# Unmasked cross attention: scores and maxima as three one-pass products instead of one fp32 product

## The reference, cut to what matters

```
q = x @ Wq.T + bq
k = context @ Wk.T + bk
v = context @ Wv.T + bv
# split in 16 heads
scores = jnp.einsum('bhtd,bhcd->bhtc', q, k) / jnp.sqrt(d)      # d = 16
attn = jax.nn.softmax(scores, axis=-1)
out = jnp.einsum('bhtc,bhcd->bhtd', attn, v) @ Wo.T + bo
```

## Time and profile before

| | |
|---|---|
| median of 3 runs | 5438.19 us (5427.34 to 5443.7) |
| profiled execution, own time | 5452.68 us |
| its span | 5450.7 us |
| PE busy in the span | 4830.3 us (89%) |
| PE weight loads busy | 3801.2 us (70%) |
| DVE busy | 2680.2 us (49%) |
| ACT (ScalarE) busy | 2135.3 us (39%) |
| POOL (GpSimd) busy | 589.6 us (11%) |
| mean granted TensorE clock | 0.929 of 2.4 GHz |

### The profile page before, as it was taken

How to read it: one execution, slowest core, us unless ns; L and a number is a source line. 1 busy time by engine, 2 the same in 40 slices (tenths; PEclk the granted TensorE clock), 3 DMA queues, 4 the chain that set the end, 5 groups by cost and what they waited for, 6 DMA issues and landing times. The chain is left out here.

```text
span 5450.7 us, 148101 instructions
## 1 busy us (share of the span) xinstructions
PE 4830.3 (89%) x66180; PEld 3801.2 (70%) x66180; DVE 2680.2 (49%) x4650; ACT 2135.3 (39%) x4116; POOL 589.6 (11%) x375
## 2 busy tenths in 40 slices
PE   6999989499999699999886799999459969999968
PEld 5877867388888578887455377877348858888844
DVE  4555545466666445554344255555255545555531
ACT  3554532233333344444021144554225534444430
POOL 1111111000000111110310011110110011111000
PEclk9999985699999899999997899999769989999979
DMA  1111100311111111110000111110101111111000
GB/s 62 39 44 39 39 10 6 89 47 50 50 47 47 50 40 40 40 40 16 32 16 16 35 38 39 39 39 26 22 22 53 51 58 40 40 40 40 22 8 26
DMA packets 82376, 203.70 MB, mean 37 GB/s; under 512 B 26864, under 2 KB 42096, under 8 KB 81760
## 3 DMA queue, kind: packets, MB, share of 16 engines
q1 hardware_dynamic: 81792, 194.79, 11.5%
HBM read 188.06 MB, written 6.70 MB: 36 GB/s over the span
## 5 line engine op out<-in xcount | busy, mean ns | idle before, releaser
L678 DVE TENSOR_REDUCE x_pm<-banks 128x4 f32<-128x1536 f32 (+2 forms) x512 | 935.3, 1827 | 691.7 <-PE banks L581 691.7
L775 ACT ACTIVATE x_pl<-banks 128x384 f32<-128x384 f32 x1536 | 628.8, 498 | 710.8 <-PE banks L564 710.8
L505 POOL TENSOR_TENSOR x_cl<-xnT,x_ch 128x1601 fp32r<-128x1601 f32 x120 | 400.6, 3338 | 3744.5 <-ACT x_ch L790 3744.5
L780 ACT ACTIVATE x_kT<-banks,x_bk 128x384 f32<-128x384 f32 (+2 forms) x512 | 305.1, 596 | 557.0 <-PE banks L592 557.0
L592 PE MATMUL banks<-x_ch,x_wh 128*128 128x384 f32 (+2 forms) x1024 | 409.6, 400 | 92.6 <-POOL x_v L512 89.8
L564 PE MATMUL banks<-x_q,x_kT 32*128 32x128 f32 x13312 | 485.2, 277 | 6.0 <-issue 5.9
L602 PE MATMUL banks<-x_wh,x_ch 128*128 128x256 f32 (+1 forms) x1664 | 489.1, 294 | 0.0
L581 PE MATMUL banks<-x_kT,x_q 32*128 32x384 f32 (+2 forms) x4096 | 456.5, 512 | 13.6 <-DVE x_v L710 8.9
L602 PE MATMUL banks<-x_wh,x_cl 128*128 128x256 f32 (+1 forms) x1664 | 467.8, 281 | 0.0
L602 PE MATMUL banks<-x_wl,x_ch 128*128 128x256 f32 (+1 forms) x1664 | 466.6, 280 | 0.0
L564 PEld LDWEIGHTS banks<-x_q,x_kT 32*128 32x128 f32 x13312 | 438.6, 185 | 9.7 <-issue 7.3
(11 more groups left out here) (349 smaller groups left out, 8300.0 us busy)
## 6 DMA issues: line engine op xcount, KB each, us to landing
xnT<-in_ctxT SPq DMA_DIRECT2D x120, 800.5 KB, 4.4
e_w<-in_L_pack SPq DMA_DIRECT2D x91, 384.0 KB, 3.1
e_w<-in_L_pack SPq DMA_DIRECT2D x56, 320.5 KB, 2.9
actT<-in_ctxT SPq DMA_DIRECT2D x8, 800.5 KB, 7.0
routed_rows<-rw SPq DMA_DIRECT2D x8, 512.0 KB
e_rw<-routed_rows SPq DMA_DIRECT2D x8, 512.0 KB, 8.1
x_side<-mask_rows SPq DMA_DIRECT2D x128, 12.5 KB
x_tok<-in_x SPq DMA_DIRECT2D x1, 1024.0 KB, 5.5
```

The source lines that it names most:

```text
L505: nc.gpsimd.tensor_tensor(cl[:, u, k, 0:CTX], staged(b, k), ch[:, u, k, 0:CTX], ALU.subtract).then_inc(low_done, 1)
L678: nc.vector.tensor_reduce(pm[:, c, :, g], src[:, :, 0:hi - lo], AX.X, ALU.max).then_inc(max_done, 1)
L775: nc.scalar.activation(probabilities(c, j, lo, hi).rearrange("p t q -> p (t q)"), mine[j][:, 0:(hi - lo) * P], ACT.Exp).then_inc(exp_done, 1)
L780: nc.scalar.activation(kT[:, c, lo:hi], mine[1 if g == 0 and inside(b if c else b - 1) else 0][:, 0:hi - lo], ACT.Identity, bias=col[:, c: ...
```

## The change

In unmasked calls, `kT` becomes `kh` and `kl`, and `qb` becomes `qh` and `ql`, all F32R. ScalarE writes `kh` where it wrote `kT`. A new DVE step `take_k` writes `kl` = projected keys + bias - `kh`, from the PSUM bank that ScalarE reads too, after it waited for `k_taken`; it comes right after `take_max` in each cycle, before `divide`, `take_output` and `take_v`. TensorE's `wait_free` waits for the new semaphore `k_low` in place of `k_taken`. `take_q` has four instructions where it had two, the last two wait for the first two. Each score product and each maximum product becomes three, with four strips inside and the three products outside.

```diff
-        kT = net.sb(tag + "_kT", [P, KC, CTX], ctx=mem)
+        if masked:
+            kT = net.sb(tag + "_kT", [P, KC, CTX], ctx=mem)
+        else:
+            kh = net.sb(tag + "_kh", [P, KC, EVEN], F32R, ctx=mem)
+            kl = net.sb(tag + "_kl", [P, KC, EVEN], F32R, ctx=mem)
...
-                after(pe, k_taken, *keys_by(k))
+                after(pe, k_taken if masked else k_low, *keys_by(k))
...
-                    for j in range(4):
-                        r = slice(32 * j, 32 * j + 32)
-                        last = nc.tensor.matmul(sets[g % 2][j][0:n, (t - lo) * P:(t - lo + 1) * P], kT[r, c, t * P:t * P + n],
-                                                qb[r, u, c], start=False, stop=True, skip_group_check=True)
+                    for keys, q in ((kT, qb),) if masked else ((kh, qh), (kh, ql), (kl, qh)):
+                        for j in range(4):
+                            r = slice(32 * j, 32 * j + 32)
+                            last = nc.tensor.matmul(sets[g % 2][j][0:n, (t - lo) * P:(t - lo + 1) * P],
+                                                    keys[r, c, t * P:t * P + n], q[r, u, c], start=False, stop=True,
+                                                    skip_group_check=True)
...
+                else:
+                    even = hi + hi % 2
+                    for n, (q, keys) in enumerate(((qh, kh), (ql, kh), (qh, kl))):
+                        for j in range(4):
+                            r = slice(32 * j, 32 * j + 32)
+                            last = nc.tensor.matmul(into[j][:, 0:even - lo], q[r, u, c], keys[r, c, lo:even], start=(n == 0),
+                                                    stop=(n == 2))
...
+            def take_k(unit, c, g, bank):
+                lo, hi = KEYS[g]
+                hi += hi % 2
+                dve.wait_ge(k_taken, unit + 1)
+                nc.vector.scalar_tensor_tensor(kl[:, c, lo:hi], bank[:, 0:hi - lo], col[:, c:c + 1], kh[:, c, lo:hi], ALU.add,
+                                               ALU.subtract).then_inc(k_low, 1)
+
             def take_q(b, u):
+                if not masked:
+                    src = qT[:, :, bass.ds(b * S, S)]
+                    for e in range(2):
+                        nc.vector.tensor_scalar(qh[:, u, :, e * S:(e + 1) * S], src, net.parity[:, 12 + e:13 + e], None,
+                                                ALU.mult).then_inc(q_staged, 1)
+                    for e in range(2):
+                        dve.wait_ge(q_staged, 4 * b + e + 1)
+                        nc.vector.scalar_tensor_tensor(ql[:, u, :, e * S:(e + 1) * S], src, net.parity[:, 12 + e:13 + e],
+                                                       qh[:, u, :, e * S:(e + 1) * S], ALU.mult,
+                                                       ALU.subtract).then_inc(q_staged, 1)
+                    return
...
+                        if not masked and inside(b + 1):
+                            take_k(k + 8, c, g, mine[1 if g == 0 and inside(pb) else 0])
                         if g == 1 and c == 0 and inside(b - 1):
                             divide(b - 1, mine[3])
```

More of the change, by code:

```diff
@@ L383, in cross_attention @@
     names = ("w_in bias_in raw_in0 raw_in1 w_high w_low high_done low_done pad_set mask_in0 mask_in1 side_set shift_set "
-             "sums_set q_staged m_full max_done z_step z_ready z_turned nm_ready s_full exp_done k_full k_taken v_full "
+             "sums_set q_staged m_full max_done z_step z_ready z_turned nm_ready s_full exp_done k_full k_taken k_low v_full "
              "v_taken pv_full o_taken den_full inverted out_ready")
@@ L388, in cross_attention @@
             side_set, shift_set, sums_set, q_staged, m_full, max_done, z_step, z_ready, z_turned, nm_ready, s_full,
-            exp_done, k_full, k_taken, v_full, v_taken, pv_full, o_taken, den_full, inverted, out_ready):
+            exp_done, k_full, k_taken, k_low, v_full, v_taken, pv_full, o_taken, den_full, inverted, out_ready):
         raw_in, mask_in = (raw_in0, raw_in1), (mask_in0, mask_in1)
@@ L400, in cross_attention @@
         late_p = net.sb(tag + "_pl", [P, 4, KEY_TILES - EARLY, P], ctx=mem)
-        qb = net.sb(tag + "_q", [P, 2, KC, P], ctx=mem)
+        if masked:
+            qb = net.sb(tag + "_q", [P, 2, KC, P], ctx=mem)
+        else:
+            qh = net.sb(tag + "_qh", [P, 2, KC, P], F32R, ctx=mem)
+            ql = net.sb(tag + "_ql", [P, 2, KC, P], F32R, ctx=mem)
         side = net.sb(tag + "_side", [P, 2, PADDED], F32R, ctx=mem) if masked else None
@@ L569, in maxima @@
                 if c == 0 and g == 0:
-                    pe.wait_ge(q_staged, 2 * b + 2)
+                    pe.wait_ge(q_staged, 2 * b + 2 if masked else 4 * b + 4)
                     if masked:
@@ L578, in maxima @@
                         nc.tensor.matmul(into[j][:, 0:even - lo], ones_r[r], side[r, u, lo:even], start=True, stop=True)
[L579 to L582, removed]
+                    for j in range(4):
+                        r = slice(32 * j, 32 * j + 32)
+                        last = nc.tensor.matmul(into[j][:, 0:hi - lo], qb[r, u, c], kT[r, c, lo:hi], start=False, stop=True,
+                                                skip_group_check=True)
+                else:
+                    even = hi + hi % 2
+                    for n, (q, keys) in enumerate(((qh, kh), (ql, kh), (qh, kl))):
+                        for j in range(4):
+                            r = slice(32 * j, 32 * j + 32)
+                            last = nc.tensor.matmul(into[j][:, 0:even - lo], q[r, u, c], keys[r, c, lo:even], start=(n == 0),
+                                                    stop=(n == 2))
                 last.then_inc(m_full, 1)
@@ L779, in one @@
                             act.wait_ge(k_full, k + 9)
-                            nc.scalar.activation(kT[:, c, lo:hi], mine[1 if g == 0 and inside(b if c else b - 1) else 0][:, 0:hi - lo],
+                            if not masked:
+                                hi += hi % 2
+                            nc.scalar.activation((kT if masked else kh)[:, c, lo:hi], mine[1 if g == 0 and inside(b if c else b - 1) else 0][:, 0:hi - lo],
                                                  ACT.Identity, bias=col[:, c:c + 1]).then_inc(k_taken, 1)
```

## The result

The changed kernel takes 5495.7 us (median of 4 runs, 5493.4 to 5504.8) against 5440.9 us before (4 runs): ratio 1.0104, 95% interval 1.0076 to 1.0132. It is slower by 55 us; 5497 was forecast. The profiled execution took 5494.93 us, with a span of 5492.9 and a granted clock of 0.931 (0.929 before), so the clock has no part in it. The profiled executions themselves lie 42 us apart (5452.68 before, 12 above the median of its runs).

What follows compares the result with a forecast made beforehand. TensorE's queue was taken as the bound; costlier scores, shorter maxima and DVE's delay at `divide` summed to +1.84 us a batch, +59 us over 16 batches and 2 calls, from 5438.2 to 5497 us, range 5445 to 5535.

Steps and rivals of the forecast that it cites:

- What bounds: Unmasked calls: TensorE's queue is the bound, matmul busy 646 of 700 us, with no cold clock to win back.
- the cycles from 672.80 and 677.19: Three-tile cycles where maxima and exponential end together: shift products to key projection 2.07 us, +0.33 and +0.31.
- Scores: Score products: a third round per tile adds 0.11 us, 0.33 in three-tile cycles and 0.44 in four-tile ones.
- The full round at 0.111: Score products: a one-pass round of four strips is load-bound and costs 0.11 us, like an fp32 round.
- The shift products: Before the scores: 0.28 us for 384 columns, about 0.11 of it an exposed weight load, left in.
- The rival that it goes: Exposed load behind the shift products disappears: up to 0.11 us in each of 8 cycles, 5469 us; chance 0.25.
- Maxima: Maximum products: three one-pass instructions last 0.70 us instead of 0.81; gains count only where maxima end after the exponential.
- The 512-key cycles: Cycles from 660.11 and 681.62, where maxima end last: -0.07 and +0.04 us up to the key projection.
- DVE: `take_k` takes 0.55 us, mostly in idle time; only the `divide` cycle pays, +0.41; longer `take_q` fits in 0.74 idle.
- the third rival: DVE becomes the bound: `take_k` costs 0.9 us and delays `take_v` in all cycles, 5532 us; chance 0.1.
- The sum: All cycles: +1.84 us a batch x 16 batches x 2 calls = +59 us, 5497 us on the median.
- The fast rival: One-pass score rounds run at streaming speed: -1.26 us a batch, -40 us, 5398 us; chance 0.13.

Runs made afterwards that it cites:

- both half runs: Changed kernel's scores with 64 stationary columns in each full tile (5457 us), or with 64 of the 128 moving columns (5500.7 us); one run each.
- the square: Changed kernel with scores and maxima each fp32 or one-pass, ratios to before: both fp32 1.0042, only maxima one-pass 1.0010, only scores one-pass 1.0129, both 1.0104.

## Why the prediction was right, and where its terms were off

**What bounds.** TensorE's queue, by the shape of the cycle: confirmed. In the cycles from 672.80 and 677.19 the added time of the scores comes through (0.27 and 0.22 from start to start), and the shorter maxima bring 0.03 at most.

**Scores.** The full round at 0.111 read off L553 came out exactly, and both half runs show that the load is the reason. Two sizes were off. I priced the last tile, which has 65 keys, like the others: there the three rounds take 0.18 together where two fp32 ones took 0.22, so twice a batch +0.11 was charged for about nothing. The load length that I had read from these very 65 columns said so. And the first round of each group takes 0.06; hence 2.00 and 2.01 instead of 2.07 in the cycles from 672.80 and 677.19. Both make the forecast too dear.

**The shift products.** Leaving the 0.28 in was right. My reading of it, a load of the scores that is exposed by rows or by format, was wrong; the runs exclude both. The rival that it goes fell with that.

**Maxima.** 14 to 17 us, by the square. The 512-key cycles gained 0.17 and 0.15 up to the projection where -0.07 and +0.04 were forecast: their maxima end 0.84 after they start, as worked out, but they start 0.16 to 0.20 earlier. From start to start 0.11 and 0.01 of that were kept.

**DVE.** The term that was too small: 0.41 at `divide` against 0.49 measured, and 0.70 where the maxima are fp32. `take_k` takes 0.62 rather than 0.55 and lengthens DVE's chain by 0.70, of which the shorter maxima give back 0.2, as forecast. The longer `take_q` went into the 0.74 of idle time, also as forecast. That DVE becomes the bound everywhere, the third rival, didn't come: in the other cycles whose loads are shown above TensorE waits for the exponential.

**The sum.** In the shortest cycles the terms give +1.59 us a batch, not 1.84: 51 us, not 59. The other 5 come from what I had not priced. The mean of the periods lies 1.33 us above the shortest one where it lay 0.96 above it before: pauses of TensorE with no releaser in the profile, such as this one in the middle of a score group (timeline of TensorE, after):

```profile
675.11 0.22 PE L573 MATMUL banks<-x_qh,x_kl 32*128 32x128 f32 x1 [0.34 <-issue]
```

Most of them stand in the attend, in the four-tile cycles (waits of TensorE: total us, times, longest; the stretches 30 to 790 and 3160 to 3900 us before, then after):

```profile
PE banks L611 <- issue: 8.2, 6, 1.5
PE banks L611 <- issue: 8.7, 6, 2.0
PE banks L628 <- issue: 10.3, 11, 2.0
PE banks L628 <- issue: 11.1, 10, 2.0
```

With the other lines they come to 21.7 us before and 26.7 after, in one execution of each. What they come from stays open. So 56 against 59 is partly luck: scores were overpriced by some 0.4 us a batch, DVE underpriced by 0.1, and pauses left out.

**The fast rival** rested on one-pass loads that overlap or go faster. The Trainium skill (TensorE: Matmul & The Clock Gate, weight-path perf modes) states a faster load for full-width weights that are not FP32, by reading 32 bits at a time, with no win for fp32 itself. For F32R the trace shows no win either: the loads of L573 last 190 ns in fp32 (the masked calls) and 190 ns in F32R (high parts), and a strip's round stays at 0.11.

## What to carry to other kernels

Count weight loads, not passes: in these runs a product in row groups cost the longer of its load (128 stationary columns: 0.11 us for a round of four) and its stream, so three one-pass products with 128 moving columns cost half as much again as the two instructions of an fp32 product, while with 322 to 512 moving columns they were cheaper. Look for a form that the kernel already has (here L553) before pricing a new one, and price odd sizes (the 65-key tile) on their own. Where only a shift is wanted, as for a softmax's maximum, one one-pass product does: here it was worth 50 us. And read a gain from the start of one stage to the start of the next, over many repetitions: one batch, measured up to the projection, had two terms off, by 0.10 and 0.15, and the right sum.

## What the runs showed that I had not expected

- A round's start-to-start is the same 0.11 us with 64 and with 128 moving columns, and 0.06 with 64 stationary ones (0.11 and 0.06 also for 128 and 65): with 128 stationary columns the streaming is hidden but for the last round's.
- The gap of 0.28 us behind shift products of 384 columns stays for 4 and 32 rows, and for fp32 and one-pass products behind it.
- A wait can carry the wrong name: 0.70 us of the maxima is put down to ScalarE where DVE's chain ends 0.26 us before it is over.
- `take_k` lasts 0.62 us and costs DVE's chain 0.70; taking a multiply of 0.29 out of it brings `take_v` forward by 0.33.
- The period's mean exceeds its shortest value by 0.96 us before (first 13 periods of each call), by 1.33 after and by 0.38 with one maximum product; the pauses are not in proportion to TensorE's instructions. With half the load in the scores it is 2.60.
